# Whole fp32 products for the shared expert and the router, and rows kept once, in a decoder layer on one core

## The reference, cut to what matters

```python
logits = (flat @ router_w).astype(jnp.float32) + router_bias
probs = jax.nn.softmax(logits, axis=-1)
top_w, top_i = jax.lax.top_k(probs, TOPK)
...
gate = jax.lax.conv_general_dilated(x_ncw, conv_w, window_strides=(1,), padding=[(KS - 1, 0)], dimension_numbers=('NCW', 'OIW', 'NCW'))
gate = jnp.transpose(gate, (0, 2, 1))
shared = jax.nn.silu(gate) * (hidden_states @ shared_up_w) @ shared_down_w
return shared + routed
```

## Time and profile before

| | us |
|---|---|
| median of 3 runs | 891.41 (889.56 to 891.85) |
| the profiled execution | 891.68 |
| its span, first to last instruction | 889.9 |
| PE busy | 710.0 (80% of the span) |
| DVE busy | 697.6 (78%) |
| ACT busy | 424.3 (48%) |
| POOL busy | 409.8 (46%) |
| mean granted PE clock | 0.906 |

### The profile page before, as it was taken

The page is one execution under the profiler, slowest core; times in us unless marked ns, Lnnn a source line. Parts: engine busy times, 40 slices in busy tenths (PEclk is TensorE's granted clock), DMA queues, the critical chain, the costliest instruction groups (busy, mean ns, idle before and its releaser), DMA issues. The chain is left out here.

```text
span 889.9 us, 13382 instructions
## 1 busy us (share of the span) xinstructions
PE 710.0 (80%) x4332; PEld 542.7 (61%) x4332; DVE 697.6 (78%) x1160; ACT 424.3 (48%) x698; POOL 409.8 (46%) x433
## 2 busy tenths in 40 slices
PE   4665886778868878678768979999999987989960
PEld 3353543456435554446336869998898975778850
DVE  4599999999999999999997756668768573554316
ACT  4666587454883738955542523433433321144420
POOL 1074585654856648677860122221233224315660
PEclk9868797798986989889989999999999999899985
DMA  6032011220112101144100211332321119745418
GB/s 180 0 87 57 24 26 46 49 48 15 33 37 60 42 14 42 36 110 114 48 1 7 75 49 64 122 122 87 120 97 50 61 54 285 182 130 155 140 31 283
DMA packets 58306, 70.80 MB, mean 80 GB/s; under 512 B 14101, under 2 KB 43224, under 8 KB 58238
## 3 DMA queue, kind: packets, MB, share of 16 engines
q1 hardware_dynamic: 42878, 50.99, 20.9%
q10 hardware_dynamic: 11616, 10.76, 3.8%
q0 software_dynamic: 3744, 8.19, 2.7%
HBM read 36.54 MB, written 18.66 MB: 62 GB/s over the span
## 5 line engine op out<-in xcount | busy, mean ns | idle before, releaser
L236 POOL TENSOR_TENSOR pu<-ut,bt 128x512 f32<-128x512 f32 x256 | 275.9, 1097 | 160.5 <-PE ps L590 139.5
L449 DVE TENSOR_TENSOR_SCAN h<-da,hlast,ps 128x512 f32<-128x512 f32 x256 | 307.2, 1256 | 3.8 <-PE ps L590 3.8
L590 PE MATMUL ps<-ident,pu 128*128 128x128 f32 x1024 | 170.7, 304 | 78.2 <-DVE h L449 74.0
L590 PEld LDWEIGHTS ps<-ident,pu 128*128 128x128 f32 x1024 | 128.7, 156 | 165.7 <-issue 85.5
L335 ACT ACTIVATE da<-dt_rep,neg_a 128x512 f32<-128x512 f32 x256 | 174.1, 716 | 97.8 <-DVE h L449 97.2
L575 PE MATMUL ps<-h,pick 128*32 128x512 f32 x512 | 77.6, 682 | 2.2 <-DVE h L449 2.2
L861 POOL DMA_INDIRECT rows_by_token<-yt,yrow x46 | 44.7, 972 | 51.3 <-DVE yrow L1234 24.1
L1015 DVE TENSOR_TENSOR p_lo<-ps,p_hi 128x512 fp32r<-128x512 f32 x64 | 35.1, 587 | 40.3 <-ACT p_hi L872 40.2
L1272 PE MATMUL ps<-v_hi,p_hi 128*128 128x256 f32 x208 | 59.7, 287 | 1.2 <-DVE x_res L1128 1.2
L1272 PE MATMUL ps<-v_hi,p_lo 128*128 128x256 f32 x208 | 58.5, 281 | 0.0
L1272 PE MATMUL ps<-v_lo,p_hi 128*128 128x256 f32 x208 | 58.5, 281 | 0.0
(11 more groups left out here) (244 smaller groups left out, 1467.3 us busy)
## 6 DMA issues: line engine op xcount, KB each, us to landing
dt_rep<-dt SPq DMA_DIRECT2D x256, 64.0 KB, 2.0
mask_sb<-in_mask_BxSxS_ik_dram SPq DMA_DIRECT2D x16, 800.5 KB, 4.4
xt<-rows_by_expert SPq DMA_DIRECT2D x46, 129.0 KB
rows_by_token<-pad ACTq DMA_DIRECT2D x4, 1024.0 KB, 5.1
yb<-rows_by_token SPq DMA_DIRECT2D x4, 512.0 KB, 5.2
yb<-rows_by_token ACTq DMA_DIRECT2D x4, 512.0 KB, 5.9
x_res<-in_x_dram SPq DMA_DIRECT2D x1, 1536.0 KB, 7.2
c_raw<-in_ctx_dram SPq DMA_DIRECT2D x1, 1536.0 KB
```

Source lines behind the costliest of these rows:

```text
L236: pool.tensor_tensor(pu[:, t % NPU, :, :].rearrange("p t (n d) -> p t n d", n=QC), ut[:, q % 2, :, 32 * b:32 * b + 32].unsqueeze(2).to_bro ...
L449: dve.tensor_tensor_scan(h[:, QC * (s % NH) + j, :], da[:, t % NDA, :], psU[:, t % NU, :], hlast[:, k:k + 1], ALU.mult, ALU.add).then_inc( ...
L590: last = pe.transpose(psU[:, t % NU, i * P:(i + 1) * P], pu[:, t % NPU, i, :], ident[:, :])
```

## The change

The split of `x3`, of the shared weights and of `t1` goes. There is one fp32 `x3`, copied once by ACT (`x3_copy`), one fp32 `cv` for the convolution weights, and the shared weights are used where they were loaded (`sh_raw`). Each group of three float32r products is one fp32 matmul; the router's logits use one fp32 matmul per half in place of two. `t1` has two buffers, and `h_high` and `h_low` are gone. `xt` has a place of its own, and SP no longer waits for `up_ps`.

```diff
+                t1 = sb("t1", [P, 2, BANK], F32, use)
                 with ExitStack() as begin:
                     cv_raw = sb("cv_raw", [P, DM, KS], F32, begin)
-                h_hi, h_lo = sb("h_hi", [P, BANK], F32R, use), sb("h_lo", [P, BANK], F32R, use)
             yb = sb("yb", [P, YB, HALF, 2 * DM], F32, second)
             w_all = sb("w_exp", [P, NX, WE], F32, second)
             done = sb("done", [P, NTILE, NX], F32, second)
@@ -682,7 +680,7 @@
         filled, scores_ps, masked, nb_ready, exp_done = sem("filled"), sem("scores_ps"), sem("masked"), sem("nb_ready"), sem("exp_done")
         pt_ps, pthi_ready, ptlo_ready, pv_ps = sem("pt_ps"), sem("pthi_ready"), sem("ptlo_ready"), sem("pv_ps")
...
             sp_.wait_ge(tab_ready, 2)
-            sp_.wait_ge(up_ps, NCH)
             sp_.wait_ge(rows_in, 16 * 2 * NT)
             sp_.wait_ge(pads_in, 16 * NX)
             for s in range(NPAIR):
...
-            def x3_high(t):
+            def x3_copy(t):
                 act.wait_ge(x3_ps, t + 1)
-                act.activation(x3_hi[:, :, ds(t * P + KS - 1, P)], psA[:, 0:KE * P].rearrange("p (k n) -> p k n", k=KE),
-                               ACT.Copy).then_inc(x3hi_ready, 1)
+                act.activation(x3[:, :, ds(t * P + KS - 1, P)], psA[:, 0:KE * P].rearrange("p (k n) -> p k n", k=KE),
+                               ACT.Copy).then_inc(x3_ready, 1)
...
-            def h_high(c):
-                act.wait_ge(t1_ready, c + 1)
-                if c:
-                    act.wait_ge(down_ps, c)
-                act.activation(h_hi[:, :], t1[:, :], ACT.Copy).then_inc(hhi_ready, 1)
-
             act.wait_ge(pv_ps, NT)
-            x3_high(NT - 1)
+            x3_copy(NT - 1)
             silu(0)
-            h_high(0)
             act.wait_ge(bv_added, NT)
             for e in ACT_EXPERTS:
                 load_expert(act, e)
             silu(1)
-            h_high(1)
             act.wait_ge(tab_ready, 1)
             for e in range(ACT_PADS):
                 write_pad(act, e)
             for c in range(2, NCH):
                 silu(c)
-                h_high(c)
             route_exp(NCH - 1)
...
-            dve.memset(x3_hi[:, :, 0:KS - 1].bitcast(U32), 0)
-            dve.memset(x3_lo[:, :, 0:KS - 1].bitcast(U32), 0)
+            dve.memset(x3[:, :, 0:KS - 1], 0.0)
...
-            def split_conv(k):
+            def conv_copy(k):
                 dve.wait_ge(cv_ps, k + 1)
-                dve.tensor_copy(cv_hi[:, :, k, :], cv_src[k]).then_inc(shared_split, 1)
-                dve.wait_ge(shared_split, 2 * k + 3)
-                dve.tensor_tensor(cv_lo[:, :, k, :], cv_src[k], cv_hi[:, :, k, :].bitcast(F32), ALU.subtract).then_inc(shared_split, 1)
-
-            def split_shared():
-                dve.wait_ge(shared_in, 48)
-                dve.tensor_copy(sh_hi[:, :], sh_raw[:, :]).then_inc(shared_split, 1)
-                dve.wait_ge(shared_split, 1)
-                dve.tensor_tensor(sh_lo[:, :], sh_raw[:, :], sh_hi[:, :].bitcast(F32), ALU.subtract).then_inc(shared_split, 1)
+                dve.tensor_copy(cv[:, :, k, :], cv_src[k]).then_inc(cv_ready, 1)
...
                 p_low(i, 0, 2)
-                if on(i, -3):
-                    x3_low(i - 3)
                 p_low(i, 2, NGRP)
...
                 if i == NT:
-                    split_shared()
                     for k in range(KE):
-                        split_conv(k)
+                        conv_copy(k)
...
             def gated(c):
                 dve.wait_ge(up_ps, c + 1)
                 dve.wait_ge(sg_ready, c + 1)
-                if c:
-                    dve.wait_ge(h_ready, c)
-                dve.tensor_tensor(t1[:, :], sg[:, c % 2, :], bank[2 + c % 2], ALU.mult).then_inc(t1_ready, 1)
-
-            def h_low(c):
-                dve.wait_ge(hhi_ready, c + 1)
-                dve.tensor_tensor(h_lo[:, :], t1[:, :], h_hi[:, :].bitcast(F32), ALU.subtract).then_inc(h_ready, 1)
+                if c >= 2:
+                    dve.wait_ge(down_ps, c - 1)
+                dve.tensor_tensor(t1[:, c % 2, :], sg[:, c % 2, :], bank[2 + c % 2], ALU.mult).then_inc(t1_ready, 1)
 
             def shared_add(c):
                 dve.wait_ge(down_ps, c + 1)
@@ -1199,23 +1165,18 @@
                     last = dve.tensor_tensor(rows, bank[6 + r].rearrange("p (n d) -> p n d", n=2), rows, ALU.add)
                 last.then_inc(shared_added, 1)
 
-            x3_low(NT - 1)
             gated(0)
             route_logits(NCH - 1)
             route_top(NCH - 1)
-            h_low(0)
             route_rank(NCH - 1)
             route_rows(NCH - 1)
             dve.tensor_copy(pad_row[:, :], base[:, :]).then_inc(tab_ready, 1)
             gated(1)
             route_table()
-            h_low(1)
             shared_add(0)
             gated(2)
-            h_low(2)
             shared_add(1)
             gated(3)
-            h_low(3)
             shared_add(2)
             shared_add(3)
             route_weights(NCH - 1)
...
             def logits(c):
-                pe.wait_ge(x3lo_ready, CHT * (c + 1))
+                pe.wait_ge(x3_ready, CHT * (c + 1))
                 if c == 0:
                     pe.wait_ge(r_in, 32)
                 for t in range(CHT):
                     cols = slice(KS - 1 + (CHT * c + t) * P, KS - 1 + (CHT * c + t + 1) * P)
-                    parts = [(k, part) for k in range(KE) for part in (x3_hi, x3_lo)]
-                    for n_, (k, part) in enumerate(parts):
-                        last = pe.matmul(psR[:, t * NE:(t + 1) * NE], part[:, k, cols].bitcast(F32), r_w_raw[:, k, :],
+                    parts = list(range(KE))
+                    for n_, k in enumerate(parts):
+                        last = pe.matmul(psR[:, t * NE:(t + 1) * NE], x3[:, k, cols], r_w_raw[:, k, :],
                                          start=(n_ == 0), stop=(n_ == len(parts) - 1))
                 last.then_inc(lg_ps, 1)
...
@@ -1445,8 +1406,7 @@
                     pe.wait_ge(sg_ready, c - 1)
                 for n_, (tap, k) in enumerate(todo):
                     cols = slice(c * BANK + tap, (c + 1) * BANK + tap)
-                    last = products(bank[c % 2], (cv_hi[:, tap, k, :], cv_lo[:, tap, k, :]), (x3_hi[:, k, cols], x3_lo[:, k, cols]),
-                                    n_ == 0, n_ == len(todo) - 1)
+                    last = pe.matmul(bank[c % 2], cv[:, tap, k, :], x3[:, k, cols], start=(n_ == 0), stop=(n_ == len(todo) - 1))
                 last.then_inc(gate_ps, 1)
 
             def up(c):
@@ -1454,21 +1414,19 @@
                     pe.wait_ge(t1_ready, c - 1)
                 for k in range(KE):
                     cols = slice(KS - 1 + c * BANK, KS - 1 + (c + 1) * BANK)
-                    last = products(bank[2 + c % 2], (sh_hi[:, k * FI:(k + 1) * FI], sh_lo[:, k * FI:(k + 1) * FI]),
-                                    (x3_hi[:, k, cols], x3_lo[:, k, cols]), k == 0, k == KE - 1)
+                    last = pe.matmul(bank[2 + c % 2], sh_raw[:, k * FI:(k + 1) * FI], x3[:, k, cols], start=(k == 0), stop=(k == KE - 1))
                 last.then_inc(up_ps, 1)
 
             def down(c):
-                pe.wait_ge(h_ready, c + 1)
+                pe.wait_ge(t1_ready, c + 1)
                 if c:
                     pe.wait_ge(shared_added, c)
                 for t in range(CHT):
                     rows = slice(t * P, (t + 1) * P)
-                    last = products(bank[6 + t // 2][:, t % 2 * DM:(t % 2 + 1) * DM], (h_hi[:, rows], h_lo[:, rows]),
-                                    (sh_hi[:, KE * FI:], sh_lo[:, KE * FI:]), True, True)
+                    last = pe.matmul(bank[6 + t // 2][:, t % 2 * DM:(t % 2 + 1) * DM], t1[:, c % 2, rows], sh_raw[:, KE * FI:], start=True, stop=True)
                 last.then_inc(down_ps, 1)
 
-            pe.wait_ge(shared_split, 2 * KE + 2)
+            pe.wait_ge(cv_ready, KE)
             gate(0)
             x3_transposed(NT - 1)
             up(0)
@@ -1618,15 +1576,14 @@
         scan_block(nc, ins["x"], w_attn, x_res, stats2, (w_in_hi, w_in_lo, xnT_hi, xnT_lo), load_next, clear_context, make_pad,
                    ident, power, ps)
         with ExitStack() as tail:
-            tile_bufs = (sb("xt", [P, XT, 2, ROW], F32, tail),
-                         sb("xT", [P, 2, KE * 2 * P], F32, tail),
...
-        x3_lo = sb("x3_lo", [P, KE, KS - 1 + SEQ], F32R)
+        x3 = sb("x3", [P, KE, KS - 1 + SEQ])
+        xt = sb("xt", [P, XT, 2, ROW])
```

More of the change, by code:

```diff
@@ L692, in attend_and_route @@
         w_exp_in = sem("w_exp_in")
[L693 to L695 removed]
+        shared_in, cv_ps, cv_ready = sem("shared_in"), sem("cv_ps"), sem("cv_ready")
+        gate_ps, up_ps, sg_ready, t1_ready, down_ps, shared_added = (
+            sem("gate_ps"), sem("up_ps"), sem("sg_ready"), sem("t1_ready"), sem("down_ps"), sem("shared_added"))
         xt_in = [sem(f"xt_in{i}") for i in range(XT)]
@@ L887, in step @@
                 if on(i, -3):
```

(20 more changed lines are left out.)

11 lines of the change are left out of this document (3 added, 8 removed).

## The result

| | kernel before | changed kernel |
|---|---|---|
| median of the runs | 891.78 us (889.56 to 894.37, 6 runs) | 876.67 us (874.61 to 879.52, 6 runs) |
| ratio, 95% interval | | 0.9831 (0.9802 to 0.9860) |
| profiled execution | 891.68 us, span 889.9 | 879.27 us, span 877.5 |

The change takes 15 us, 1.7%. The forecast was 882.0 us in a range of 874.5 to 888.0: right in sign and range, 5.3 us too slow. The time is nearest to that of rival (a), 875.4, in which the hole goes.

The account below looks back on a forecast made before the run. PE was taken to bound the attention steps and expert tiles, with a held-up stretch between them where no engine is full. Logits 8.4, the stage before the tiles 0.8 and early `xt` 0.5 off 891.7 gave 882.0 us, range 874.5 to 888.0.

Parts of the forecast that it names:

- rival (a): Before the expert tiles: the hole goes and ACT's loads bound; 7.4 us in place of 0.8, 875.4 us; chance 0.20.
- the hole: The 7.8 us between the end of PE's last chunk 3 logits matmul and DVE's addition waiting for it; releaser unknown.
- Step 1: Router logits in attention steps, 16 of 32 rows go: 1.74 us for chunks 0 and 1, 4.87 for chunk 2.
- Step 2: The 16 `x3_low` on DVE and PE's wait for them, in the attention steps: removal taken to gain nothing.
- Steps 3 and 4: Splits ahead of gate(0) go, 1.9 to 2.0 us earlier; fp32 matmuls cost PE 6.4 us more over four chunks.
- Step 5: Stage up to the first expert tiles: hole about as before, PE's extra work eats shorter ends; gain 0.8 us.
- T: Time of DVE's addition of chunk 3's logits, which ends the hole: taken as 752.4, between 751.5 and 753.4.
- Step 6: `xt` early at the first expert tiles: second pair's 0.65 us lateness goes, less 0.15 for ACT's copy; gain 0.5 us.
- (b): Rival: PE's clock falls in the attention steps all the same; 2.7 us less gain, 884.7 us; chance 0.12.
- (c): Rival: before the tiles, the hole lasts until the experts' weights have landed; some 5.6 us more, 887.6; chance 0.10.
- (d): Rival: PE's clock stays at half under the fp32 matmuls after the hole; 19.5 us more, 901.5; chance 0.04.

Follow-up runs that it names:

- e1: Kernel before with router logits from the high part of the rows alone, 16 matmul rows for 32 per chunk: 885.52 us, ratio 0.9895.
- e8: Changed kernel with DVE's addition of chunk 3's logits made to wait for gate(1) as well: 882.74 us, ratio 0.9860 to the kernel before.
- e3: Changed kernel with SP's wait for the last up matmuls put back ahead of the tile-row loads: 881.75 us, ratio 0.9849 to the kernel before.
- e2: Changed kernel with each router-logits matmul made twice, 32 rows per chunk: 892.65 us, ratio 0.9973 to the kernel before.
- e6: Changed kernel with three of ACT's six expert loads moved ahead of its copy of tile 15's rows: 879.52 us, ratio 0.9845 to the kernel before.
- e9: Kernel before with all fifteen experts' loads on SP's queue and none on ACT's: 894.74 us, single run.
- e5: Kernel before with both queues' expert loads held back until DVE has read chunk 3's logits: 902.17 us, single run.
- e7: Changed kernel with each gate matmul of 512 columns made as two of 256: 880.61 us, single run.

## Why the prediction was right, and where it was not

**Step 1, logits.** Right. 1.74 us were worked out for each of chunks 0 and 1, 2.03 and 2.10 came, of which e1 puts 1.8 on the logits. Chunk 2 gave 4.86 for 4.87, clock fall and all. The row of 0.109 us decided rightly: by "Back-to-back issue gap" of the Trainium skill's page "TensorE: Matmul & The Clock Gate" a chunk would have given 0.4 to 1.0 us, and the trace disagrees; by the section "LDWEIGHTS" of that page of the Trainium skill it is 0.107 us a row, and the trace agrees (0.106).

**Step 2, `x3_low`.** Taken as nothing. With the logits' share off, 0.2 to 0.3 us for each four steps remain (52.27 in e1, 52.06 in the changed kernel). Below what the timed runs can tell, but not nothing. Which wait it came out of is not shown: PE waits 0.3 to 0.4 us for DVE's `p_lo` or `base` once in some steps, in both kernels.

**Steps 3 and 4, ahead of chunk 3's logits.** 1.9 us from the splits, less 1.3 for the slower gate(0) and up(0), make 0.6; 0.92 was measured. gate(0) stands right behind the transposes, at 728.31, and 12 rows go from 736.94 to 742.18 in gate(1): 0.437 us each for 0.43; down(0) took 1.72 us for 1.73.

**Step 5 failed**, in its first choice: that the hole stays and the stretch hangs on it (T = 752.4). The stretch from the maximum behind chunk 2's logits to the first tiles gained 6.2 us, where the forecast had 0.8 and rival (a) 7.4. e8 gives an estimate of how much of that is the hole. With a delay of 8.3 us put back the tiles came at 174.03 us from chunk 0's logits; 185.37 less that, less the 8.99 us gained up to that maximum, leaves 2.35 us for the stage. So two terms were mis-sized besides. T was to be 752.4 in old times. e8's addition stands at 145.02 us, and with the 8.99 added back at 154.01, against 156.43 before: T = 751.5, the early end of the range, which is luck, since the experiment set it. And from T on it took 29.0 us, not 29.6. Together 1.5 us, from 0.8 to 2.35. The rest, 3.8 us (3.0 by the second profile of the changed kernel), would be the hole's price up to the first tiles: about half of its 7.8 us, because ACT's loads bound the stretch as soon as it is gone. Two things stay open. The profiles that this compares are of different chips. And why the profile of the changed kernel has no hole is not known; that the change removed it is not shown, so the step failed on a term whose cause the runs did not find.

**Rival (a)** had the order of what follows once the hole is gone, though not a reason for its going: `silu(1)` behind ACT's loads, the table, `shared_add(0)`, down(1). Shifted by the 6.1 us between the two maxima (720.27 and 714.15), `silu(1)` at 746.97 is 753.1 for its 754.1, the table's last row ended at 759.8 for 760.8, and the tiles began at 776.6 for 775.4. What it lacked is the half clock behind PE's wait: down(1) took 2.8 us for 1.7, gate(3) 5.9 for 5.2. Its chance of 0.20 looks too low. The prediction had seen that nothing in the code explains the hole, and then let the same 45 loads and a DMA share of 1.08 decide for its staying; the changed kernel has both (1.09) and no hole. A delay that nothing explains should have been held as likely to go as to stay, from one profile to the next.

**Step 6** was wrong in sign, by little. The rows of the second pair were late by 1.07 us, not in time: the padding rows land later against PE than before, as PE now comes earlier. The wait that was removed had been covered by them (e3).

**(b)** did not come; e2 shows what it would have been, and more: 3.2 us in chunk 1 and 1.5 in chunk 2, beyond the rows themselves. **(c)** and **(d)** did not come. After the wait for `shared_add(0)` the clock was at half from 755.8 to 759.2.

## What to carry to other kernels

Price each matmul by the row it occupies in the trace, not by its columns: a matmul row of 16 columns with a block of 128 weights of its own took 0.106 to 0.109 us here, so halving the count halved the time (3.48 us to 1.69). A stretch that hangs on a delay without a named releaser should be worked out twice, with it and without, and the difference is not the delay's length but the distance to what is late next. Where transfers saturate a stretch, moving one of their issues forward moved the wait to the next reader (e6). And before a delay is put down to the kernel, profile both kernels on the same chip: here every profile whose chip is known goes by its chip, with a delay or without, and the kernel is only one possible cause.

## What I had not expected of the hardware

- A signal from PE can reach its waiter up to 7.8 us after the matmul ended, while PE itself works on (gate(1) ran its full length meanwhile). Several late signals arrive together: three within 0.23 us in the kernel before, for matmuls that ended over 2.8 us. In these profiles a delay was there in 9 of the 13 that had expert loads under way. Those nine are all eight profiles of chips 5 and 10 and the first of the kernel before, and each lacks records. It repeats within 0.1 us for one kernel (7.77 and 7.84) and not for another (3.98 and 2.49). Its cause stays open: a second queue is not needed (e9), and e5 and e7 leave the rest undecided.
- The clock fell to half within runs of 16-column matmuls 2.4 us behind their start (before, chunk 2) and 2.6 us (e2, chunk 1), yet in other chunks the same 32 rows ran at full clock. With half the rows it did not fall in the steps, in any of nine profiles.
- The same wait of 1.9 us ahead of gate(0) left the clock full in the kernel before, and at half for 3.4 us in e1. What came before differs: in the kernel before the clock had been at half from 708.0 to 714.9 and full since, in e1 it had been full throughout. Whether that is the reason was not tried.
